# A two-layer Perceiver kernel: the spectral attention's bias as a one-row product, its spectra taken off by ScalarE, and the first half's spectra and roots moved within the last attention unit

## The chip, the cores and the metric

The kernel runs on one core of a Trainium2 chip. The metric is the device time of one execution in microseconds (us). Engines are named as the profile names them: PE is TensorE (PEld its weight loads), ACT is ScalarE, DVE is VectorE, POOL is GpSimd, SP is SyncE, which here only issues DMAs. L1563 is line 1563 of the kernel before.

## The reference

Two Perceiver layers on x [2, 256, 256] with a context [2, 4096, 256]. In order: cross attention with a Gelu, latent attention, a mixture of experts, a masked cross attention with 16 heads of 16 over the 4096 context rows, then the spectral attention that the change touches, and a mixture of expert projections with causal attention. The spectral attention, cut:

```python
def unit_projection(x):
    f = fft(x); f = f / (abs(f) + 1e-8); return ifft(f).real
query  = unit_projection(x @ Wq.T + bq)
keys   = unit_projection(x @ Wk.T + bk)
values = unit_projection(x @ Wv.T + bv)
s   = cumsum(bind(keys, values), axis=1)      # bind: product of the spectra
out = unbind(s, query)                        # product with the conjugate
x = x + out                                   # its input is layernorm(x)
```

## The kernel before, in words

Tokens lie as four tiles of 128 rows; tiles 0 and 1 are the first half (batch 0), tiles 2 and 3 the second (batch 1). Each engine has an instruction list written out by hand, and they meet at semaphores, so an engine takes its work strictly in the order of its list.

The masked cross attention runs as 32 units, one per batch and head. PE's `unit` has four turns `j`; each does score groups 2j and 2j+1 (`score_half` L1446, `score_mask` L1455) and two groups of the products with the values (`values_group` L1467); ACT takes one exponential for each half group (L953, 16 in a unit). The two last value groups of the last unit stand behind it. ACT copies the sums of a finished unit (`sums_out` L919), PE turns them (`sum_rows` L1478), DVE divides (`rows_out` L2169), and when a batch has all 16 heads, PE transposes (`o4_T` L1532), ACT copies (`o4T_out` L924) and PE projects (`y4_rows` L1542), eight products in all for a half.

From there on each half runs through: add to x (`add_psum` L2214), layer norm (`layer_stats` L1814, a power on POOL L667, `layer_scale` L1827), a transpose (`batch_norm_T` L1551) and its copy by ACT (`batch_norm_out` L930), and `spectra` (L1563), a product with the projection weights already multiplied by the Fourier matrix (`fold`), 258 columns of real and imaginary parts. k = 0, 1, 2 are keys, values and queries of the first half, k = 3, 4, 5 those of the second. Each spectrum is two tiles by two chunks of the contraction, and each of these four products stands as two MATMUL instructions in the trace. Behind a spectrum DVE adds the bias row out of a copy broadcast over the partitions and stores it (`spectrum_out` L2232), ACT squares (`squares` L939), DVE adds the two parts (`magnitude` L2240), ACT takes the root (`roots` L973). DVE then multiplies keys and values (`bind` L2245 to L2250), scales by the reciprocal sizes (`key_sizes`, `invert` L2267, `scale_keys` L2273), PE makes running sums (`running_sums` L1635, L1634), DVE multiplies with the conjugate query (`unbind`, again L2245 to L2250), PE transposes (`o5_T` L1643), ACT copies (`o5T_out` L978), PE returns by the inverse transform (`inverse` L1653), and DVE adds (`add_inverse`, L2214 again).

The first half's `spectra(0)` to `spectra(2)` run on PE inside the last unit, by the function `last_unit`, which `unit` calls in each turn after the first score group and at the turn's end. The second half waits for the last unit's sums. Behind it all stands the last stage: `project` (L1674) on PE and `gather` (L2419 to L2423) on DVE, the first `gather` behind the second half's `layer_scale(8)`. `spin` (L1052) are idle products that only keep PE running.

Of the kernel before, what the change touches and what calls it, by code (L numbers as in the profile page):

```python
# [165 lines left out]
def build(nc, a, out):  # L166
    ctx = ExitStack()
    with ctx:
# [570 lines left out]
        def _(act):  # L739
# [193 lines left out]
            def squares(k):  # L933

                b, n = k // 3, k % 3
                act.wait_ge(spec_ready, k + 1)
                if k >= 2:
                    act.wait_ge(mag_ready, k - 1)
                nc.scalar.activation(mag[:, QT * (k % 2):QT * (k % 2) + QT, :], spec[:, n, b * QT:(b + 1) * QT, :], ACT.Square)\  # L939
                   .then_inc(square_ready, 1)  # L940

            def softmax_numerators(s, u, first=False, last=False):
                for n in range(HALVES):
                    if n == 0 and last:
                        o4T_out(0)
                    if n == 4 and not first:
                        sums_out(s - 1, u - 1)
                    if n == 10 and last:
                        batch_norm_out(3, 0, T5[0])
                    if n == 14 and last:  # L950
                        squares(0)
# [8 lines left out]
            for s in range(RING):  # L960
                softmax_numerators(s, U4 - RING + s, last=(s == RING - 1))
            squares(1)
            sums_out(RING - 1, U4 - 1)
            squares(2)
            act.wait_ge(in_gate, 16 * DC + 32)
# [14 lines left out]
            roots(0)  # L980
            roots(1)
            o4T_out(1)
            roots(2)
            batch_norm_out(4, 1)
            squares(3)
            o5T_out(0)
            squares(4)
            roots(3)
            roots(4)
            squares(5)  # L990

            def row_squares(b):
# [53 lines left out]
        def _(pe):  # L1046
# [435 lines left out]
            def unit(s, u, fills, first=False, left=3, between=None):  # L1482
# [24 lines left out]
                for j in range(PAIRS):  # L1507
# [5 lines left out]
                    if between is not None:  # L1513
                        between(j, False)
                    score_group(2 * j + 1)
                    if j == PAIRS - 1 and left >= 1:
                        negmax_T(u + 1)
# [5 lines left out]
                    if between is not None:  # L1523
                        between(j, True)

# [29 lines left out]
            def spectra(k):  # L1555
# [4 lines left out]
                for q in range(QT):  # L1560
                    t = b * QT + q
                    for c in range(DC):
                        last = mm(bank[:, SPEC5[k] + q, 0:2 * NF], xnT[:, c, t * P:(t + 1) * P], fold[:, n, c, :],  # L1563
                                  start=(c == 0), stop=(c == DC - 1))
                last.then_inc(spec_psum, 1)

            def last_unit(j, whole):

                if j == 0 and whole:
                    y4_rows(0, 0)  # L1570
                    y4_rows(0, 1)
                elif j == 2 and not whole:
                    batch_norm_T(xn5[0], 5, T5[0])
                elif j == 2:
                    pe.wait_ge(in_w5, 16 * N_W5[2])
                    pe.wait_ge(xnT_ready, 4)
                    spectra(0)
                    spectra(1)
                elif j == 3 and whole:
                    spectra(2)  # L1580
# [226 lines left out]
        def _(dve):  # L1807
# [400 lines left out]
            link(v.tensor_tensor(x[:, :, :], x[:, :, :], bo4.unsqueeze(1).broadcast_to([P, TT, D]), ALU.add))  # L2208
            rows_out(RING - 1, U4 - 3)

# [5 lines left out]
            add_psum(0, Y5[0])  # L2216
            layer_stats(halves[0])
            dve.wait_ge(in_gate, 16 * DC + 32)
            v.tensor_tensor(sim2, sim6, sim6, ALU.mult).then_inc(sim_sq, 1)
# [3 lines left out]
            def rows(b):  # L2223

                return slice(b * QT, (b + 1) * QT)

            def spectrum_out(k):

                b, n = k // 3, k % 3
                o = SPEC5[k]  # L2230
                dve.wait_ge(spec_psum, k + 1)
                v.tensor_tensor(spec[:, n, rows(b), :], bank[:, o:o + 2, 0:2 * NF],  # L2232
                                brow[:, n, :].unsqueeze(1).broadcast_to([P, QT, 2 * NF]), ALU.add).then_inc(spec_ready, 1)

# [67 lines left out]

            spectrum_out(0)
            spectrum_out(1)
            magnitude(0)
            bind(0)
            magnitude(1)
            spectrum_out(2)
            rows_out(0, U4 - 2)
# [6 lines left out]
            link(v.reciprocal(col6[:, 3, :], col6[:, 2, :]))  # L2316
            key_sizes(0)
            invert(1, 0)
# [7 lines left out]
            scale_queries(0)  # L2326
            spectrum_out(3)
            unbind(0)
            spectrum_out(4)
            magnitude(3)  # L2330
# [4 lines left out]
            link(v.reciprocal(root6[:, TT:], root6[:, TT:]))  # L2335
            spectrum_out(5)
            add_inverse(0)
# [224 lines left out]
```

## Time and profile before

| | |
|---|---|
| median of 3 runs | 973.49 us (970.43 to 975.55) |
| the profiled execution | 974.15 us |
| its span, first to last instruction | 972.5 us |
| mean granted TensorE clock | 0.979 |
| busy share: PE, DVE, ACT, POOL | 94%, 61%, 46%, 10% |
| last unit of the cross attention | about 838 to 861 us of the span |
| spectral attention, both halves, to the first `gather` | to 907.3 us |
| last stage | 907.3 to 972.5 us |

A row of the timeline gives start and length in us, the engine, the line, the operation with its tensors, how many instructions it merges, and in brackets how long the engine sat idle before it and what released it. `bank` is PSUM, `region` the large SBUF tensor. Granted clock 1.00 is 2.4 GHz, 0.50 is 1.2 GHz.

### The profile page before, as it was taken

Reading aid. Unit: us, or ns where it says so; the run is one execution under the profiler, and the core shown is the slowest. Engines: PE = TensorE matmul, PEld = TensorE weight load, DVE = VectorE, ACT = ScalarE, POOL = GpSimd, SP = SyncE. Lnnn points to the kernel's source line nnn. Section 1 sums busy time; section 2 is a strip of 40 time slices with the busy share of each in tenths; the row PEclk is TensorE's granted clock in tenths of the full one; section 3 lists DMA queues with packets and bytes.
Section 4 is the critical chain, followed back from the end, with each engine's and each line's share of the span. In section 5 each row is a group of like instructions: output and inputs, shape, how many; then the busy total and the mean of one; then the engine's idle time right before and its main releaser. Section 6 shows DMA issues by size and latency. Waiting matters only on the chain.

```text
span 972.5 us, 20335 instructions
## 1 busy us (share of the span) xinstructions
PE 916.6 (94%) x7344; PEld 533.9 (55%) x7346; DVE 593.6 (61%) x1554; ACT 450.0 (46%) x836; POOL 96.9 (10%) x132
## 2 busy tenths in 40 slices
PE   5999989999989998499999999999999999978998
PEld 5888876556556556334444444444444444456657
DVE  3455343664422225478777777778777777468883
ACT  3444433541012224456666666666666666632102
POOL 1222321000501110100000000000000000010000
PEclk9999998999999999889999999999999999989999
DMA  7844689507118208974445544555445552710000
GB/s 260 272 164 162 223 320 304 165 1 260 58 24 119 77 21 210 248 193 75 68 64 81 80 67 64 69 80 78 64 59 80 80 71 70 132 44 1 1 0 22
DMA packets 76358, 107.75 MB, mean 111 GB/s; under 512 B 27084, under 2 KB 62512, under 8 KB 72275
## 3 DMA queue, kind: packets, MB, share of 16 engines
q1 hardware_dynamic: 71147, 91.65, 43.6%
q0 software_dynamic: 4960, 14.96, 4.2%
q8 instruction: 34, 0.56, 0.3%
q10 hardware_dynamic: 200, 0.44, 0.2%
q14 instruction: 17, 0.14, 0.0%
HBM read 84.21 MB, written 21.03 MB: 108 GB/s over the span
## 4 chain that ended last, share of the span: by engine, by line
PE 81%; DVE 8%; DMA 4%; ACT 2%; POOL 2%; issue 2%; SPq 0%; ACTq 0%; POOLq 0%; DVEq 0%
PE bank L1446 14%; PE bank L1467 13%; PE bank L1455 9%; PE bank L1424 7%; PE bank L1091 5%; PE bank L1306 5%; PE bank L1104 5%; PE bank L1334 3%; PE bank L1674 2%; PE bank L1186 1%; PE bank L1079 1%; PE bank L1736 1%; PE bank L1195 1%; PE bank L1478 1%; DMA keys_split<-region 1%
## 5 line engine op out<-in xcount | busy, mean ns | idle before, releaser
L953 ACT ACTIVATE region<-bank 128x512 f32<-128x512 f32 x512 | 278.0, 595 | 161.1 <-PE bank L1455 161.1
L2140 DVE CUSTOM_DVE_ANT_0 xnT<-bank,region 128x1024 bf16<-128x1024 f32 x128 | 156.2, 1220 | 81.3 <-issue 81.3
L1446 PE MATMUL bank<-region 128*128 (+1 forms) x1024 | 158.8, 277 | 2.1 <-ACT region L953 1.5
L2140 DVE CUSTOM_DVE_ANT_0 region<-bank,region 128x1024 bf16<-128x1024 f32 x128 | 156.3, 1221 | 0.9 <-issue 0.5
L1467 PE MATMUL bank<-region 128*32 128x256 f32 x2048 | 138.8, 385 | 0.0
L1446 PEld LDWEIGHTS bank<-region 128*128 128x128 bf16 x1024 | 69.8, 98 | 120.6 <-issue 59.6
L1455 PE MATMUL bank<-region,identb 64*64 64x512 bf16 x1024 | 105.7, 403 | 0.0
L1424 PE MATMUL bank<-region,xnT 64*128 64x512 bf16 x248 | 76.2, 387 | 8.8 <-DMA xnT<-region 8.5
L1467 PEld LDWEIGHTS bank<-region 128*32 128x32 f32 x2048 | 58.8, 109 | 40.5 <-ACT region L953 14.5
L1426 PE MATMUL bank<-region,xnT 64*128 64x512 bf16 x248 | 76.2, 387 | 0.0
L1306 PE MATMUL bank<-region 128*64 (+1 forms) x192 | 59.8, 466 | 2.2 <-DVE region L2053 1.6
L1091 PE MATMUL bank<-xnT,region 128*128 128x256 f32 x256 | 58.1, 380 | 0.3 <-ACT xnT L743 0.3
L722 POOL COPY region<-region 128x512 f32<-128x512 f32 x30 | 18.5, 617 | 398.5 <-PE bank L1467 398.5
L1104 PE MATMUL bank<-region 128*128 128x256 f32 x256 | 57.9, 379 | 0.0
L1455 PEld LDWEIGHTS bank<-region,identb 64*64 64x64 bf16 x1024 | 28.9, 103 | 48.9 <-issue 48.0
L1091 PEld LDWEIGHTS bank<-xnT,region 128*128 128x128 f32 x256 | 48.7, 191 | 6.9 <-issue 0.4
L1912 DVE TENSOR_TENSOR region<-region 128x1024 bf16<-128x1024 f32 x16 | 19.6, 1226 | 52.1 <-ACT region L784 52.1
L1104 PEld LDWEIGHTS bank<-region 128*128 128x128 f32 x256 | 47.5, 190 | 5.8
L779 ACT ACTIVATE region<-bank 128x512 f32<-128x512 f32 x32 | 19.1, 598 | 63.7 <-PE bank L1091 63.7
L677 POOL DMA_DIRECT2D keys_split<-region x48 | 35.9, 749 | 102.2 <-DVE region L1912 102.2
L1674 PE MATMUL bank<-region,xnT 128*128 128x384 f32 x128 | 43.8, 490 | 1.0 <-ACT xnT L930 0.8
L1306 PEld LDWEIGHTS bank<-region 128*64 128x64 f32 (+1 forms) x192 | 29.6, 159 | 27.0 <-issue 6.3
(376 smaller groups left out, 1196.8 us busy)
## 6 DMA issues: line engine op xcount, KB each, us to landing
region<-keys_split SPq DMA_DIRECT2D x224, 128.0 KB, 4.9
region<-in_ctx SPq DMA_DIRECT2D x32, 512.0 KB, 7.0
keys_split<-region POOLq DMA_DIRECT2D x48, 256.0 KB, 4.4
region<-in_L_ffn_we_gate SPq DMA_DIRECT2D x8, 688.0 KB
region<-in_L_ffn_we_up SPq DMA_DIRECT2D x8, 688.0 KB
region<-in_mask_1x1xSxS_ik SPq DMA_DIRECT2D x1, 4096.0 KB, 15.9
region<-in_L_ffn_we_down SPq DMA_DIRECT2D x8, 512.0 KB
mask_kept<-region SPq DMA_DIRECT2D x1, 2048.0 KB, 12.1
```

The costliest lines, as they stand in the source:

```text
L677: pool.dma_start(keys_dram[part, bass.ds(b * D, D), bass.ds((2 * j + s) * CH, CH)] .rearrange("(c p) f -> p c f", p=P), split[s][:, part, ...
L953: nc.scalar.activation(prob4[n % PROBS].rearrange("p a b -> p (a b)"), bank[:, SCORE4[n], :], ACT.Exp, scale=SCALE4).then_inc(exp4_ready, 1)
L1091: last = mm(bank[:, 2 + p, t * S:(t + 1) * S], ctxT[s % 2][:, d, f:f + P], xnT[:, d, b * S:(b + 1) * S], start=(d == 0), stop=(d == DC - 1))
L1104: last = mm(bank[:, 4 + q, 0:D], geluT[p][:, t, q * P:(q + 1) * P], ctx_in[s][:, 2 * p + t, :], start=(s + p + t == 0), stop=(s == SLOTS1 ...
L1306: last = mm(bank[0:rows_by(i), 2 * w + n, 0:FH], xbT[i % 2][:, c, 0:rows_by(i)], packed3[:, bass.ds(owner, 1), at3:at3 + FH].rearrange("p ...
L1424: mm(bank[:, b, :], qmax4[s][0:64, q * P:(q + 1) * P], slab[s][0:64, c * CH:(c + 1) * CH], start=True, stop=True)\
L1426: mm(bank[:, b + 1, :], qmax4[s][64:P, q * P:(q + 1) * P], slab[s][64:P, (c + 1) * CH:(c + 2) * CH], start=True, stop=True).then_inc(max_p ...
L1446: mm(bank[:, SCORE4[n], k * S:(k + 1) * S], slab[s][:, t * P:(t + 1) * P], qT4[:, bass.ds(u, 1), :].rearrange("p o q -> p (o q)"), start=( ...
L1455: last = mm(bank[o, SCORE4[2 * g + k], :], identb[i, i], maskT[i, 4 * g + 2 * k:4 * g + 2 * k + 2, :].rearrange("p a b -> p (a b)"), start ...
L1467: last = mm(bank[32 * k:32 * k + 32, 7, 0:S], vaug[s % 2][:, 4 * g + k, :], prob4[(2 * g + k // 2) % PROBS][:, k % 2, :], start=(g == 0), ...
L1674: last = mm(bank[:, DEEP6[k % len(DEEP6)], 0:2 * QKV], xnT[:, c, t * P:(t + 1) * P], w6[:, c, e:e + 2, :].rearrange("p a b -> p (a b)"), s ...
L2140: v.tensor_tensor_reduce(out=junk[q], in0=bank[:, 3 + 2 * q:5 + 2 * q, :].rearrange("p a b -> p (a b)"), in1=maskN[:, q, 2 * c * CH:2 * (c ...
```

## The change

1. The bias comes in as one more product: `ones[0:1, :]` (one row of 128 ones) with the bias row `brow[0:1, n, :]` of 258 columns opens each accumulation, two for a spectrum, twelve in all. As each float32 product stands as two MATMULs in the trace, that is 24 instructions.
2. DVE's `spectrum_out` (six of them) is gone. ACT squares straight from PSUM and then copies the spectrum out, two ACT instructions where one was.
3. In the last unit, PE's pieces stand earlier: `y4_rows` in turn 0 between the two score groups, `batch_norm_T` in turn 1, `spectra(0)` and `spectra(1)` at the end of turn 1, `spectra(2)` at the end of turn 2.
4. On ACT, `squares(0)` and `squares(1)` with their copies stand among the last unit's exponentials; behind the last exponential come `roots(0)`, `roots(1)`, then `squares(2)` and its copy, and only then `sums_out` of the last unit.
5. On DVE, `rows_out` of unit 29 stands behind the first half's statistics, `magnitude(1)` ahead of `bind(0)`, and `key_sizes(0)` ahead of the `rows_out` of the last two units.

```diff
             def squares(k):
-                b, n = k // 3, k % 3
-                act.wait_ge(spec_ready, k + 1)
+                act.wait_ge(spec_psum, k + 1)
                 if k >= 2:
                     act.wait_ge(mag_ready, k - 1)
-                nc.scalar.activation(mag[:, QT * (k % 2):QT * (k % 2) + QT, :], spec[:, n, b * QT:(b + 1) * QT, :], ACT.Square)\
-                   .then_inc(square_ready, 1)
+                nc.scalar.activation(mag[:, QT * (k % 2):QT * (k % 2) + QT, :], bank[:, SPEC5[k]:SPEC5[k] + 2, 0:2 * NF],
+                                     ACT.Square).then_inc(square_ready, 1)
+
+            def spectrum_out(k):
+
+                b, n = k // 3, k % 3
+                nc.scalar.activation(spec[:, n, b * QT:(b + 1) * QT, :], bank[:, SPEC5[k]:SPEC5[k] + 2, 0:2 * NF], ACT.Copy)\
+                  .then_inc(spec_ready, 1)
...
             for s in range(RING):
                 softmax_numerators(s, U4 - RING + s, last=(s == RING - 1))
-            squares(1)
-            sums_out(RING - 1, U4 - 1)
-            squares(2)
...
             roots(0)
             roots(1)
+            squares(2)
+            spectrum_out(2)
+            sums_out(RING - 1, U4 - 1)
             o4T_out(1)
             roots(2)
             batch_norm_out(4, 1)
-            squares(3)
+            for k in (3, 4):
+                squares(k)
+                spectrum_out(k)
             o5T_out(0)
-            squares(4)
             roots(3)
             roots(4)
             squares(5)
+            spectrum_out(5)
...
                 for q in range(QT):
                     t = b * QT + q
+                    mm(bank[:, SPEC5[k] + q, 0:2 * NF], ones[0:1, :], brow[0:1, n, :], start=True, stop=False)
                     for c in range(DC):
                         last = mm(bank[:, SPEC5[k] + q, 0:2 * NF], xnT[:, c, t * P:(t + 1) * P], fold[:, n, c, :],
-                                  start=(c == 0), stop=(c == DC - 1))
+                                  start=False, stop=(c == DC - 1))
                 last.then_inc(spec_psum, 1)
...
-                if j == 0 and whole:
+                if (j, part) == (0, 0):
                     y4_rows(0, 0)
                     y4_rows(0, 1)
-                elif j == 2 and not whole:
+                elif (j, part) == (1, 1):
                     batch_norm_T(xn5[0], 5, T5[0])
-                elif j == 2:
+                elif (j, part) == (1, 2):
                     pe.wait_ge(in_w5, 16 * N_W5[2])
                     pe.wait_ge(xnT_ready, 4)
                     spectra(0)
                     spectra(1)
-                elif j == 3 and whole:
+                elif (j, part) == (2, 2):
                     spectra(2)
...
-            spectrum_out(0)
-            spectrum_out(1)
             magnitude(0)
+            magnitude(1)
             bind(0)
-            magnitude(1)
-            spectrum_out(2)
+            key_sizes(0)
             rows_out(0, U4 - 2)
             rows_out(None, U4 - 1)
...
-            spectrum_out(3)
             unbind(0)
-            spectrum_out(4)
             magnitude(3)
             bind(1)
             magnitude(4)
...
-            spectrum_out(5)
             add_inverse(0)
```

ACT at the end of the last unit, before: L953 are exponentials, L939 the squares, L919 the copy of the last unit's sums, L973 the roots with their table load, L924 the copy of the transposed rows for the second half's projection.

```order
L953 ACTIVATE region<-bank 128x512 [waits score4] x2
L939 ACTIVATE region<-region 128x516 [waits spec_ready]
L919 ACTIVATE region<-bank 128x290 [waits o4_unit,pv_psum]
L939 ACTIVATE region<-region 128x516 [waits mag_ready,spec_ready]
L966 ACTIVATE region<-region 128x16 [waits in_gate]
L973 ACT_TABLE_LOAD
L973 ACTIVATE region<-region 128x258 [waits mag_ready] x2
L924 ACTIVATE xnT<-bank 128x2x256 [waits o4T_psum]
```

And of the change, at the same place (L962 exponentials, L938 squares, L944 the copy of the spectrum, L979 roots):

```order
L962 ACTIVATE region<-bank 128x512 [waits score4] x4
L972 ACTIVATE region<-region 128x16 [waits in_gate]
L979 ACT_TABLE_LOAD
L979 ACTIVATE region<-region 128x258 [waits mag_ready] x2
L938 ACTIVATE region<-bank 128x516 [waits mag_ready,spec_psum]
L944 ACTIVATE region<-bank 128x516
L919 ACTIVATE region<-bank 128x290 [waits o4_unit,pv_psum]
L924 ACTIVATE xnT<-bank 128x2x256 [waits o4T_psum]
```

The copy of the last unit's sums (L919) stood ahead of the table load and the roots, and now stands behind them, behind a square and behind a copy.

PE in the last turn of the last unit and behind it, before (L1446 and L1455 scores, L1467 values, L1563 a spectrum, L1478 the turn of the sums):

```order
L1446 MATMUL bank<-region 128x256
L1455 MATMUL bank<-region,identb 64x512 x4
L1467 MATMUL bank<-region 32x256 [waits exp4_ready]
L1467 MATMUL bank<-region 32x256 x3
L1467 MATMUL bank<-region 32x256 [waits exp4_ready]
L1467 MATMUL bank<-region 32x256 x3
L1563 MATMUL bank<-region,xnT 128x258 [waits spec_ready]
L1563 MATMUL bank<-region,xnT 128x258 x3
L1467 MATMUL bank<-region 32x256 [waits exp4_ready]
```

Of the change, `spectra(2)` and what follows it (L1575 the one-row product, L1577 the spectrum's own, L1457 and L1466 scores):

```order
L1575 MATMUL bank<-region,ones 128x258 [waits spec_ready]
L1577 MATMUL bank<-region,xnT 128x258 x2
L1575 MATMUL bank<-region,ones 128x258
L1577 MATMUL bank<-region,xnT 128x258 x2
L1457 MATMUL bank<-region 128x256 [waits exp4_ready]
L1457 MATMUL bank<-region 128x256
L1457 MATMUL bank<-region 128x256 [waits exp4_ready]
L1457 MATMUL bank<-region 128x256
L1466 MATMUL bank<-region,identb 64x512 x4
```

`spectra(2)` stood behind the last scores and now stands ahead of the last two score groups, and two one-row products have joined its four.

PE in the second half, of the change, from `batch_norm_T` to `o5_T`:

```order
L1564 MATMUL bank<-ident,xn 128x128 [waits xn_ready]
L1564 MATMUL bank<-ident,xn 128x128 x3
L1575 MATMUL bank<-region,ones 128x258 [waits xnT_ready]
L1577 MATMUL bank<-region,xnT 128x258 x2
L1575 MATMUL bank<-region,ones 128x258
L1577 MATMUL bank<-region,xnT 128x258 x2
L1575 MATMUL bank<-region,ones 128x258 [waits spec_ready]
L1577 MATMUL bank<-region,xnT 128x258 x2
L1575 MATMUL bank<-region,ones 128x258
L1577 MATMUL bank<-region,xnT 128x258 x2
L1657 MATMUL bank<-ident,region 128x128 [waits o5_ready]
```

Nothing has changed its place here; `spectra(3)` and `spectra(4)` are twelve products where they were eight.

## Rows read from the trace of the kernel before

**Rows 1.** The page: busy time and share of the span by engine.

```profile
PE 916.6 (94%) x7344; PEld 533.9 (55%) x7346; DVE 593.6 (61%) x1554; ACT 450.0 (46%) x836; POOL 96.9 (10%) x132
```

**Rows 2.** The chain that ended last, 838 to 975 us: start, length, what.

```profile
859.75 1.05 PE bank L1467 x16
...
861.88 1.28 ACT L973
863.17 0.73 ACT region L973 x2
864.43 3.61 PE bank L1542 x8
868.07 0.70 DVE x L2214
...
873.51 3.82 PE bank L1563 x8
877.43 0.70 DVE region L2232
```

**Rows 3.** Stretches: length, busy PE, PEld, DVE, ACT, POOL, granted clock, DMA share, GB/s.

```profile
861.00:864.00 3.00, 1.72 (x12) 1.38 (x12) 1.57 (x8) 2.97 (x7) 0.00 (x0) 1.00 0.19 62
864.00:868.00 4.00, 3.57 (x9) 2.81 (x10) 3.26 (x5) 0.69 (x2) 0.00 (x0) 0.58 0.00 0
873.00:878.00 5.00, 4.49 (x11) 3.56 (x12) 1.79 (x4) 0.46 (x1) 0.68 (x1) 0.50 0.00 0
878.00:880.00 2.00, 1.62 (x7) 1.07 (x5) 1.93 (x6) 0.63 (x1) 0.00 (x0) 0.92 0.00 0
880.00:907.00 27.00, 21.86 (x122) 17.46 (x122) 24.36 (x78) 6.40 (x14) 2.33 (x3) 1.00 0.00 1
```

**Rows 4.** Timeline of PE: spectra, `y4_rows`, `o4_T`, inverse.

```profile
842.08 1.99 PE L1542 MATMUL bank<-woutT,xnT 128*128 128x256 f32 x8
850.86 3.75 PE L1563 MATMUL bank<-region,xnT 128*128 128x258 f32 x16
862.40 0.66 PE L1532 MATMUL bank<-ident,xn 128*128 128x128 f32 x4
864.43 3.59 PE L1542 MATMUL bank<-woutT,xnT 128*128 128x256 f32 x8 [1.38 <-ACT xnT L924]
873.51 6.11 PE L1563 MATMUL bank<-region,xnT 128*128 128x258 f32 x16 [0.69 <-ACT xnT L930]
883.01 1.89 PE L1653 MATMUL bank<-region 128*128 128x256 f32 x8
```

**Rows 5.** Timeline of ACT around the last unit's end.

```profile
856.92 1.09 ACT L953 ACTIVATE region<-bank 128x512 f32<-128x512 f32 x2
860.82 0.41 ACT L919 ACTIVATE region<-bank 128x290 f32<-128x290 f32 x1 [2.29 <-PE bank L1467]
863.80 0.58 ACT L924 ACTIVATE xnT<-bank 128x512 f32<-128x512 f32 x1
```

**Rows 6.** Groups by line and form: other heights, and the instructions that change engine.

```profile
L1186 PE MATMUL bank<-region x64: 377/379/483, 165.0 to 210.9; 65*128 65x256 f32 x64
L1736 PE MATMUL bank<-region 128*128 128x256 f32 x64 | 14.8, 382 | 0.0
L2232 DVE TENSOR_TENSOR region<-bank,region 128x516 f32<-128x516 f32 x6 | 4.2, 694 | 9.5 <-PE bank L1563 9.5
L939 ACT ACTIVATE region<-region 128x516 f32<-128x516 f32 x6 | 3.8, 634 | 5.4 <-DVE region L2232 5.4
L930 ACT ACTIVATE xnT<-bank 128x512 f32<-128x512 f32 x4 | 2.4, 598 | 15.7 <-PE bank L1551 15.7
```

**Rows 7.** Timeline of DVE behind the last unit.

```profile
881.56 0.42 DVE L2245 TENSOR_TENSOR region<-region 128x258 f32<-128x258 f32 x1
885.53 0.68 DVE L2214 TENSOR_TENSOR x<-x,bank 128x512 f32<-128x512 f32 x1
907.27 0.42 DVE L2419 TENSOR_SCALAR region<-bank,weight 128x192 f32<-128x192 f32 x1
```

More of the change, by code:

```diff
@@ L947, in softmax_numerators @@
                         sums_out(s - 1, u - 1)
+                    if n == 8 and last:
+                        batch_norm_out(3, 0, T5[0])
+                        squares(0)
+                        spectrum_out(0)
                     if n == 10 and last:
-                        batch_norm_out(3, 0, T5[0])
-                    if n == 14 and last:
-                        squares(0)
+                        squares(1)
+                    if n == 12 and last:
+                        spectrum_out(1)
                     act.wait_ge(score4, HALVES * u + n + 1)
@@ L1513, in unit @@
                     if between is not None:
-                        between(j, False)
+                        between(j, 0)
                     score_group(2 * j + 1)
+                    if between is not None:
+                        between(j, 1)
                     if j == PAIRS - 1 and left >= 1:
@@ L1523, in unit @@
                     if between is not None:
-                        between(j, True)
+                        between(j, 2)
             def o4_T(b):
@@ L1561, in spectra, with last_unit @@
                     t = b * QT + q
+                    mm(bank[:, SPEC5[k] + q, 0:2 * NF], ones[0:1, :], brow[0:1, n, :], start=True, stop=False)
                     for c in range(DC):
                         last = mm(bank[:, SPEC5[k] + q, 0:2 * NF], xnT[:, c, t * P:(t + 1) * P], fold[:, n, c, :],
-                                  start=(c == 0), stop=(c == DC - 1))
+                                  start=False, stop=(c == DC - 1))
                 last.then_inc(spec_psum, 1)
-            def last_unit(j, whole):
-                if j == 0 and whole:
+            def last_unit(j, part):
+                if (j, part) == (0, 0):
                     y4_rows(0, 0)
                     y4_rows(0, 1)
-                elif j == 2 and not whole:
+                elif (j, part) == (1, 1):
                     batch_norm_T(xn5[0], 5, T5[0])
-                elif j == 2:
+                elif (j, part) == (1, 2):
                     pe.wait_ge(in_w5, 16 * N_W5[2])
@@ L2208, in _ @@
             link(v.tensor_tensor(x[:, :, :], x[:, :, :], bo4.unsqueeze(1).broadcast_to([P, TT, D]), ALU.add))
-            rows_out(RING - 1, U4 - 3)
             def add_psum(b, o):
@@ L2217, in _ @@
             layer_stats(halves[0])
+            rows_out(RING - 1, U4 - 3)
             dve.wait_ge(in_gate, 16 * DC + 32)
@@ L2225, in rows @@
                 return slice(b * QT, (b + 1) * QT)
[L2227 to L2233, printed above, removed]
             def magnitude(k):
@@ L2316, in _ @@
             link(v.reciprocal(col6[:, 3, :], col6[:, 2, :]))
-            key_sizes(0)
             invert(1, 0)
```

## The prediction

> **What bounds the kernel now.** The page comes first: PE is busy for 94% of the span, DVE for 61%, ACT for 46% [rows 1]. That is an average over stages, so the chain that ended last is read next, and in it only the stretch that the change touches [rows 2]. From the last unit's last values (859.75) the chain goes over ACT's table load and first two roots, the second half's projection on PE (864.43, L1542), DVE's addition at 868.07, spectra(3) at 873.51, and DVE's copy of that spectrum at 877.43. The stretches [rows 3] show two things: the granted clock was 1.00 up to 864 and 0.58 between 864 and 868, behind a stretch in which PE had been busy 1.72 of 3.00 us, 0.50 between 873 and 878 and 0.92 between 878 and 880; and from 880 to 907 DVE is busy 24.36 of 27 us. So the last unit is bound by PE, the middle (861 to 880) by hand-overs between ACT, PE and DVE, and 880 to 907 nearly by DVE alone. I read the change as a set of shifts of three moments: y4 of the second half done (868.02, where DVE's addition waits), bind of the second half (DVE L2245 at 881.56), and the first inverse added (885.53) [rows 7]. The last of these is followed by work that the change doesn't touch: it reaches the first gather at 907.27 [rows 7], and the last stage goes on from there. What shifts 885.53 shifts the end.
>
> **1. The one-row products in the last unit.** Each adds two MATMULs of 258 columns. No row has a height of 1. Two rows of different heights say that height doesn't count: 65 rows by 256 columns took a median of 379 ns, 128 rows by 256 columns a mean of 382 [rows 6]. Back to back, 16 instructions of a spectrum took 3.75 us, 0.234 each [rows 4]. I take 0.234 as the price of one; the lower bound is 0 (it streams beside its neighbours), and the upper is the half-clock price, 3.59/8 = 0.45 [rows 4], where the clock is down. Three spectra have 12 such instructions: 2.8 us. In the last unit PE has hardly a gap, so all of it lies on the path: the last values end at 860.80 + 2.8 = 863.6 [rows 2].
>
> **2. Where the last exponentials end.** Before, they ended at 856.92 + 1.09 = 858.01 [rows 5], with spectra(2) behind them. Now the last four wait for scores behind all three spectra: 858.01 + 2.8 + 1.9 (the own eight instructions of spectra(2), 8 x 0.234) = 862.7. The earlier y4_rows and batch_norm_T cost nothing: the same products in another order, beside exponentials that ACT has room for (it waited 2.29 us at the end of the unit [rows 5]). The new wait in ACT's list, squares(0) ahead of exponential 8, holds the exponentials back by nothing either, since the scores they need come behind spectra(1) on PE.
>
> **3. ACT ahead of the sums.** From 862.7: the gates' exponential 0.2, the table load 1.28, two roots 0.73 [rows 2], then squares(2) and its copy. These read PSUM: a copy of 512 columns from there took 598 ns, a square of 516 from SBUF 634 [rows 6], so 0.6 each, bounds 0.5 and 0.7. Together 3.4 us, and sums_out (0.41) ends at 866.5, where before it ended at 861.23 [rows 5]. That is 5.3 us later. The roots that were to come earlier come later too: 864.2 against 863.17, so key_sizes doesn't pay it back.
>
> **4. From the sums to y4.** Before, from 861.23 to 868.02: 6.8 us, of which the copy L924 lost 0.74 behind the roots (the transposes ended at 863.06, the copy began at 863.80 [rows 4, 5]). Now ACT is free there: 6.1 us, with the projection at half clock as before (3.59 us where it is 1.99 at full clock [rows 4]). y4 is done at 866.5 + 6.1 = 872.6, so this moment is **4.5 us** later. DVE's own list (two rows_out, magnitude, invert, scale_keys behind the sums) is done at about 872, just ahead of it.
>
> **5. Second half.** Call DVE's addition T (868.07 before, 872.6 now). Spectra(3) starts at T + 5.4, as before. Spectra(3) and (4) are 24 instructions where they were 16. Before, 16 took 6.11 us: 4.7 at half clock (to about 878.2) held ten, and six more at 0.234 took 1.4. With the same half-clock stretch the other 14 take 3.3: 8.0 us, to T + 13.4. Then square, copy and hand-overs, 1.4: bind(1) can start at T + 14.8, where it was T + 13.5. DVE has nothing to do meanwhile: unbind(0) no longer waits for spectra(3), is early, and DVE then idles. That is where the DVE work taken off is given back. PE goes on with o5_T 0.5, spectra(5) 12 x 0.234 = 2.8, inverse 1.9 [rows 4] and 0.2 of hand-over: T + 18.8. DVE's road to the same addition is 14.8 + (17.46 - 13.49) - 0.6 = 18.2, its spectrum_out(5) saved, so PE ends last. Before it was 885.53 - 868.07 = 17.46. So **1.35 us** later. Behind that nothing is shorter; ACT's last square and copy lie under DVE's work.
>
> The Trainium skill (TensorE: Matmul & The Clock Gate, What's actually happening) says that the half rate is the default and that activity on PE releases it; by it the longer wait before the sums (3 us now, from 863.6 to 866.5) makes a low clock at y4 surer, and eight more products make the rise behind spectra(3) no later. By that rule alone the sum stays; without the release, spectra(3) and (4) would take 24 x 0.45 = 10.8 us instead of 8.0. The granted clock of 0.50 in 873 to 878 and 1.00 from 880 [rows 3] agrees with it.
>
> **Sum.** 4.5 + 1.35 = 5.85 us on the profiled execution, 974.15 us: 980.0. The median of the runs is 0.66 lower, so 979.3. Nearly all of it is the price of the one-row products: 12 of them ahead of the sums, 8 in spectra(3) and (4), 4 in spectra(5), 24 x 0.234 = 5.6. What ACT's new order costs and what the early unbind gives almost cancel.
>
> **Rivals.** (a) *The one-row product is nearly free.* The mechanism: one row of weights and one row of data, loaded and streamed beside the tall product next to it. Then the sum is 5.85 - 5.6 = +0.2: 973.7. Not slower. It decides from about 0.19 us per instruction: under that the change is within 4.9 us. Against it: equal times for 65 and 128 rows [rows 6]; for it, only that nothing as low as 1 is shown. 0.14. (b) *The clock is held.* More products and less pause between them keep 1.00 at y4 and through spectra(3) and (4): 3.59 - 1.99 = 1.6 less, and 24 x 0.234 = 5.6 instead of 8.0, 2.4 less; DVE's list then ends last at the first place, which leaves about 1.0 of the 1.6. +2.5: 976.0, no measurable change. Against it: the pause before the sums grows. 0.15. (c) *VectorE's relief decides.* With (a) and (b) both, DVE is the bound of 868 to 907, and its three spectrum_out (3 x 0.6) and its wait for PE at 877.43 go: about -3, 970.5. This is the other side, and it needs an instruction under 0.1 us. 0.05. (d) *The clock stays low throughout*, from the sums to the end of spectra(4), because the pauses between PE's pieces are longer: 10.8 instead of 8.0, +8.6: 982.1. For it: the clock fell at 864 behind a stretch with PE busy 1.72 of 3.00 us [rows 3], and now PE stands still for 3 us there. The Trainium skill's same page says that pauses bring the default back, which is this rival's rule. 0.15. (e) The change doesn't do what it says, as where a wait on the early DMAs of fold or of the gates shows inside the unit: its price is open, 0.03.
>
> **How the numbers follow.** My forecast, +4.3 to +7.3 with 979.3 in the middle, has 0.48. A measurement of this kernel tells about 0.5% (4.9 us) from no change. Slower by more: three quarters of the forecast (0.36), all of (d) and (e), 0.54. Faster by more needs (c) and luck on top: 0.04. The rest, 0.42, is within 0.5%. The range goes from 973.5, which takes in (b) and the free product's edge, to 983.0, which takes in (d).
>
> **What would show it.** In the profile of the changed kernel: the one-row products at 0.23 us each back to back; last values at 863 to 864; PE idle for about 3 us before the turn of the sums, ACT's copy of them ending 5 us later than before; DVE idle ahead of magnitude(3) and of bind(1), 2 us or more each; the first gather at about 913; the last stage as long as before. I am wrong if the one-row products take under 0.15 us, if the first gather stands before 910, or if the clock is 1.00 between the sums and spectra(4).

## The result, and the profile after

The change is slower: 995.09 us (median of 4 runs, 986.72 to 998.9) against 974.52 us for the kernel before (970.43 to 976.99), a ratio of 1.0204 with a 95% interval of 1.0127 to 1.028. The forecast was 979.3 us with a range to 983.0, so the sign was right and the size was not. The profiled execution took 986.72 us, span 985.0, mean granted clock 0.974. It is the fastest of the four, so what the profile shows (12.6 us over the profile of before) is less than the 20.6 us between the medians. What is left is taken up behind the prediction's steps. The ratios leave out slow runs, among them those that gave the profiles of e3 (996.23 us) and e7 (998.58 us) and one run of e1 that took 4847.93 us.

The page of the changed kernel, busy time by engine (against [rows 1]):

```profile
PE 928.1 (94%) x7368; PEld 538.8 (55%) x7370; DVE 589.7 (60%) x1548; ACT 452.8 (46%) x842; POOL 96.9 (10%) x132
```

PE has 24 more instructions and is busy 11.5 us longer, which is far more than 24 times 0.234 us. The chain that ended last shows where (against [rows 2]; start, length, what):

```profile
870.92 0.70 DVE x L2227
...
881.13 1.15 PE bank L1575 x2
882.29 2.02 PE bank L1577 x4
...
894.68 3.31 PE bank L1667 x8
898.09 0.70 DVE x L2227
```

Lines of the changed kernel: L1575 is the one-row product, L1577 the spectrum's own, L1489 the turn of the sums, L1545 `o4_T`, L1657 `o5_T`, L1667 the inverse, L979 ACT's table load and roots, L938 and L944 its square and new copy. The addition at 870.92 is followed by the layer norm and the transpose; from spectra(3) at 875.91 to the addition at 898.09 the chain is all PE, with five of the six one-row pairs at 1.15 us and only the first at 0.70. The stretches (against [rows 3]; length, busy PE, PEld, DVE, ACT, POOL, granted clock, DMA share, GB/s) show why:

```profile
864.00:870.00 6.00, 5.31 (x18) 4.46 (x19) 4.05 (x11) 0.91 (x2) 0.00 (x0) 0.50 0.02 7
871.00:877.00 6.00, 2.94 (x14) 1.85 (x13) 5.14 (x12) 0.60 (x1) 3.57 (x2) 1.00 0.00 0
878.00:897.00 19.00, 19.00 (x40) 11.51 (x41) 5.30 (x15) 4.49 (x9) 0.00 (x0) 0.50 0.00 0
898.00:919.00 21.00, 17.71 (x102) 13.74 (x101) 18.61 (x61) 3.92 (x9) 2.34 (x3) 1.00 0.00 1
```

For 19 us PE has not one idle moment in the records, and all that time the clock is 0.50, that is 1.2 GHz. Before, it was back at 1.00 by 880 [rows 3]. DVE waits for it three times, in its timeline (start, length, then what; in brackets the idle time before it and what released it; against [rows 7]):

```profile
881.80 0.43 DVE L2246 TENSOR_TENSOR region<-region 128x258 f32<-128x258 f32 x1 [1.98 <-ACT region L938]
888.64 0.43 DVE L2251 TENSOR_TENSOR region<-region 128x258 f32<-128x258 f32 x1 [6.41 <-ACT region L944]
898.09 0.69 DVE L2227 TENSOR_TENSOR x<-x,bank 128x512 f32<-128x512 f32 x1 [6.12 <-PE bank L1667]
```

L2246 is magnitude(3), L2251 bind(1), L2227 the addition of the first inverse. And PE's timeline, in the last unit at full clock and in the second half at half clock (against [rows 4]; the tile forms are weights, then data):

```profile
853.67 0.70 PE L1575 MATMUL bank<-region,ones 1*128 1x258 f32 x2
854.29 1.14 PE L1577 MATMUL bank<-region,xnT 128*128 128x258 f32 x4
855.36 0.70 PE L1575 MATMUL bank<-region,ones 1*128 1x258 f32 x2
...
863.92 1.04 PE L1489 MATMUL bank<-summer,region 128*128 128x17 f32 x4 [2.73 <-ACT region L919]
...
865.65 1.09 PE L1545 MATMUL bank<-ident,xn 128*128 128x128 f32 x4
...
887.27 1.06 PE L1657 MATMUL bank<-ident,region 128*128 128x128 f32 x4
888.26 1.22 PE L1575 MATMUL bank<-region,ones 1*128 1x258 f32 x2
889.42 2.09 PE L1577 MATMUL bank<-region,xnT 128*128 128x258 f32 x4
891.44 1.22 PE L1575 MATMUL bank<-region,ones 1*128 1x258 f32 x2
...
894.47 3.50 PE L1667 MATMUL bank<-region 128*128 128x256 f32 x8
```

**One measure for all runs.** Every kernel of this study, the one before included, scatters by several us upstream of the change, so I compare profiles by one stretch: from the last unit's first `o4_T` to the first gather. It is the part that the change touches. The last stage behind it is 65.2 us long before (972.5 less 907.3) and after (985.0 less 919.8). Before, the stretch runs from 838.3 to 907.3, **69.0 us**; after, from 834.2 to 919.8, **85.6 us** (ends rounded to 0.1, so a stretch is good to 0.1). The forecast of +5.85 is 74.85 us in this measure. Its start stands in the groups of instructions by line; this is the row of before, and behind it the row of after:

```profile
L1532 PE MATMUL bank<-ident,xn x4: 272/273/327, 838.3 to 838.7; 128*128 128x128 f32 x4
```

```profile
L1545 PE MATMUL bank<-ident,xn x4: 272/272/330, 834.2 to 834.5; 128*128 128x128 f32 x4
```

### The profile page after: what moved, and what is told of

Its sections match the earlier page's. It is cut to its first block, busy times and chain, and to the rows that moved or that the text cites. A ratio compares the mean times of both kernels' runs of the same rounds, so it can differ in the third digit from the quotient of the medians.

```text
span 985.0 us, 20383 instructions
## 1 busy us (share of the span) xinstructions
PE 928.1 (94%) x7368; PEld 538.8 (55%) x7370; DVE 589.7 (60%) x1548; ACT 452.8 (46%) x842; POOL 96.9 (10%) x132
## 4 chain that ended last, share of the span: by engine, by line
PE 83%; DVE 6%; DMA 3%; SPq 3%; ACT 2%; issue 1%; another core or an unknown queue 1%; POOL 0%; ACTq 0%; DVEq 0%
PE bank L1457 14%; PE bank L1478 12%; PE bank L1466 9%; PE bank L1435 7%; PE bank L1317 6%; PE bank L1115 5%; PE bank L1102 4%; PE bank L1345 3%; PE bank L1285 2%; PE bank L1688 2%; PE bank L1577 2%; PE bank L1197 1%; PE bank L1750 1%; PE bank L1206 1%; PE bank L1489 1%
## 5 line engine op out<-in xcount | busy, mean ns | idle before, releaser
L962 ACT ACTIVATE region<-bank 128x512 f32<-128x512 f32 x512 | 277.9, 595 | 162.9 <-PE bank L1466 162.9
L1457 PE MATMUL bank<-region 128*128 (+1 forms) x1024 | 158.4, 277 | 2.1 <-ACT region L962 1.5
L1478 PE MATMUL bank<-region 128*32 128x256 f32 x2048 | 138.6, 385 | 0.0
L1457 PEld LDWEIGHTS bank<-region 128*128 128x128 bf16 x1024 | 69.7, 98 | 120.5 <-issue 59.6
L1466 PE MATMUL bank<-region,identb 64*64 64x512 bf16 x1024 | 105.7, 403 | 0.0
L1478 PEld LDWEIGHTS bank<-region 128*32 128x32 f32 x2048 | 58.9, 109 | 40.3 <-ACT region L962 14.5
L1466 PEld LDWEIGHTS bank<-region,identb 64*64 64x64 bf16 x1024 | 28.9, 103 | 48.8 <-issue 47.9
L1317 PEld LDWEIGHTS bank<-region 128*64 128x64 f32 (+1 forms) x192 | 30.3, 163 | 32.9 <-issue 12.6
L2093 DVE TENSOR_TENSOR region<-region,bank 128x344 f32<-128x344 f32 x24 | 12.3, 513 | 55.2 <-PE bank L1321 36.3
```

Source lines behind the costliest of these rows:

```text
L1317: last = mm(bank[0:rows_by(i), 2 * w + n, 0:FH], xbT[i % 2][:, c, 0:rows_by(i)], packed3[:, bass.ds(owner, 1), at3:at3 + FH].rearrange("p ...
L1457: mm(bank[:, SCORE4[n], k * S:(k + 1) * S], slab[s][:, t * P:(t + 1) * P], qT4[:, bass.ds(u, 1), :].rearrange("p o q -> p (o q)"), start=( ...
L1466: last = mm(bank[o, SCORE4[2 * g + k], :], identb[i, i], maskT[i, 4 * g + 2 * k:4 * g + 2 * k + 2, :].rearrange("p a b -> p (a b)"), start ...
L1478: last = mm(bank[32 * k:32 * k + 32, 7, 0:S], vaug[s % 2][:, 4 * g + k, :], prob4[(2 * g + k // 2) % PROBS][:, k % 2, :], start=(g == 0), ...
```

## The experiments

Three theories. **A:** products that hold fewer rows than their neighbours keep a clock that has fallen at half, though PE is busy. **B:** the new order's pauses keep it low. **C:** the one-row product is only dearer than I took it for, and the clock follows other things. All results first; "low" is the time at half clock between 840 and 925 us of the profiled execution, worked out from its mean granted clock there (two decimals, so good to 1 us); in most profiles it has a first part behind the last unit and in some a second from about spectra(3) on. Stretch and low are read from one profile each; the ratio is against the kernel before and over several runs.

| run | stretch, us | low, us | ratio (95%) |
|---|---|---|---|
| before | 69.0 | 10.2 | 1 |
| the change | 85.6 | 27.2 | 1.0204 (1.0127 to 1.028) |
| e1 bias on 128 rows | 74.7 | 13.6 | 1.0019 (0.9986 to 1.0052) |
| e2 change, no bias | 67.4 | 6.8 | 0.9978 (0.9939 to 1.0017) |
| e3 before, with one-row bias | 83.3 | 30.6 | 1.009 (1.0046 to 1.0134) |
| e4 before, with 128-row bias | 71.3 | 3.4 | 1.0025 (0.9989 to 1.0061) |
| e5 the change again | 75.2 | 3.4 | 1.0163 (1.0127 to 1.0199) |
| e6 bias on 32 rows | 86.8 | 34 | 1.0185 (1.0135 to 1.0236) |
| e7 change, with spins | 86.3 | 27.2 | 1.0118 (1.0054 to 1.0181) |
| e8 before, with spins | 65.9 | 3.4 | 0.9956 (0.9925 to 0.9988) |
| e9 128 rows in the second half only | 75.8 | 17 | 1.0096 (1.0056 to 1.0136) |
| e10 128 rows in the first half only | 84.7 | 30.6 | 1.0143 (1.0074 to 1.0211) |
| e11 128 rows and spins | 71.0 | 3.4 | 1.0052 (1.0016 to 1.0087) |
| e12 before, second spin only | 66.4 | 3.4 | 1.0017 (0.9983 to 1.005) |
| e13 bias on 64 rows | 86.8 | 34 | 1.0157 (1.0115 to 1.0199) |
| e14, e15 as e9, one run each | 73.8, 76.6 | 7, 14 | no ratio: 980.69 and 993.24 us |
| e16 as e8, again | 65.8 | 3.4 | 0.9969 (0.9937 to 1.0001) |

**e1 and e2: the bias with all 128 rows, and no bias at all.** In e1 the same sum is spread over 128 rows; all else is the change. In e2 the product is left out, so the bias is missing from what is computed.

```diff
+share = sb("share", [P, P]);  nc.gpsimd.memset(share[:, :], 1.0 / 128)
-mm(bank[...], ones[0:1, :], brow[0:1, n, :], start=True, stop=False)
+mm(bank[...], share[0:128, :], brow[0:128, n, :], start=True, stop=False)
```

> The change with its bias product 128 rows tall (a tile of 1/128 against the bias row on all 128 partitions) in place of one row; same number of instructions, same order. Theory A (one-row products keep TensorE's clock at half although PE is busy): the half-clock stretch behind spectra(3) ends within 6 us of its start, as before, and the time is 977 to 982 us, near my forecast. Theory B (the new order's pauses hold the clock down, whatever the height): as the change, 987 to 999 us, half clock for about 20 us. Theory C (only the longer time of a one-row pair, 0.62 us against 0.47, counts): about 2 us below the change.

> The change without any bias product (the bias of the spectral attention is left out). It shows what the new order and ScalarE's copies do alone. Theory A: no long half-clock stretch; 972 to 977 us, by my working +0.2 us on before. Theory B: the pauses are the same, so the clock stays down and the time is over 982 us.

With the same number of instructions of the same 258 columns, e1's stretch is 10.9 us shorter than the change's, and its time can't be told from before. PE's timeline of e1 in the second half:

```profile
884.78 1.93 PE L1579 MATMUL bank<-region,xnT 128*128 128x258 f32 x4
886.50 1.07 PE L1577 MATMUL bank<-region,share 128*128 128x258 f32 x2
...
890.81 0.60 PE L1577 MATMUL bank<-region,share 128*128 128x258 f32 x2
891.24 1.03 PE L1579 MATMUL bank<-region,xnT 128*128 128x258 f32 x4
```

The clock was down here too when spectra(3) began (1.93 us for four), and came back within the third tile, by 890: the pair at 890.81 took 0.60 us. The fall came at 883.1, just ahead of spectra(3), and lasted 6.8 us. C wanted e1 about 2 us under the change, and it is 10.9 us under it in the stretch: more than the price of the pairs is at work. e2 stands at 0.9978: the new order by itself costs nothing that can be measured. In e2's profile the clock fell only once, behind the last unit, so it doesn't show how a second fall would have ended; against B stands e1, which has the change's order and pauses and gets its clock back.

**e3 and e4: the kernel before, with the bias product alone added.** Order and `spectrum_out` as before, DVE's addition turned into a plain copy.

```diff
+mm(bank[...], ones[0:1, :], brow[0:1, n, :], start=True, stop=False)    # e3; e4: share[0:128, :], brow[0:128, n, :]
-v.tensor_tensor(spec[...], bank[...], brow[...].broadcast_to(...), ALU.add)
+v.tensor_copy(spec[...], bank[...])
```

> The kernel before, with its order and DVE's exits, but with the one-row bias product on PE, DVE copying where it added. Theory A: the half clock stays for 10 us or more from spectra(3) on, 984 us or more. Theory B: the order is the old one, so the clock comes back as before: 24 instructions at 0.23 to 0.31 us, of which the six behind the last unit's start count, 977 to 981 us.

> As the run before (old order, bias product on PE, DVE copies), with the product 128 rows tall. Both theories: 976 to 981 us; theory A expects this 5 us or more under the one-row form, theory B within 2 us of it.

The one-row product brings the long low clock into the old order as well, which is the second thing against B. With 128 rows it is gone: e4's clock fell too, 0.7 us into spectra(3), and was back after 3.4 us. A stretch of e3, then two of e4 (columns as above):

```profile
900.00:906.00 6.00, 6.00 (x13) 3.94 (x14) 2.68 (x8) 0.70 (x3) 0.00 (x0) 0.50 0.00 0
```

```profile
874.00:877.30 3.30, 3.30 (x10) 2.56 (x9) 0.54 (x2) 0.00 (x0) 0.00 (x0) 0.50 0.02 5
877.50:884.00 6.50, 5.67 (x28) 4.68 (x27) 5.79 (x15) 2.06 (x4) 0.00 (x0) 1.00 0.00 0
```

**e5: the change a second time.**

> The change unaltered, as the measure for this group's chip. All theories: 1.01 to 1.025 of before; a half-clock stretch of 15 us or more behind spectra(3) in most executions.

This profile shows that the fall is not certain. PE's timeline of e5, the same program, spectra(3) to (5):

```profile
876.27 0.66 PE L1564 MATMUL bank<-ident,xn 128*128 128x128 f32 x4 [2.37 <-DVE xn L1841]
877.61 0.70 PE L1575 MATMUL bank<-region,ones 1*128 1x258 f32 x2 [0.69 <-ACT xnT L930]
...
886.53 0.70 PE L1575 MATMUL bank<-region,ones 1*128 1x258 f32 x2
888.14 1.89 PE L1667 MATMUL bank<-region 128*128 128x256 f32 x8
```

The pauses ahead are those of after (2.37 and 0.69 us; there 2.38 and 0.69), and the clock stayed at 1.00. So one-row products don't pull a full clock down at once; where it doesn't fall, the stretch is 75.2 us, within 0.4 us of the forecast. The timed runs of e5, 978.73 to 996.87 us, are as wide as that difference and more, and the other four took 989.85 us or more: this profile, with the fastest run, is the exception.

**e6 and e13: 32 and 64 rows.** As e1, with `share[0:32, :]` at 1/32 and `share[0:64, :]` at 1/64.

> The change with the bias product 32 rows tall (a tile of 1/32 against the bias row on 32 partitions). If the height of the product is what keeps the clock down, 32 of 128 rows is still short: half clock for 10 us or more in most executions and 1.005 to 1.02 of before, between the one-row form and the 128-row form (1.002). If only height 1 is special, about 1.002.

> The bias product on 64 rows of 1/64 and 64 rows of the bias. If the rows of a product decide by degrees whether a fallen clock comes back (1 and 32 rows: stretch of 86 and 87 us; 128 rows: 75 us): 73 to 78 us from the last unit's first o4_T to the first gather, 1.000 to 1.008 of before. If anything short of 128 rows holds the clock down: 83 us or more there, 1.012 or more.

There are no degrees. Both cost what the one-row product costs. PE's timeline of e13, at full and at half clock:

```profile
848.19 0.70 PE L1577 MATMUL bank<-region,share 64*128 64x258 f32 x2
...
882.50 1.23 PE L1577 MATMUL bank<-region,share 64*128 64x258 f32 x2
```

**e7, e8, e11, e12, e16: the pauses filled.** Idle products on PE: `spin(1, 5)` (10 MATMULs) behind the second half's `o4_T` and `spin(1, 9)` (18) ahead of its `batch_norm_T`. e7 adds them to the change, e8 to the kernel before, e11 to e1; e12 has the second alone; e16 repeats e8.

```diff
 o4_T(1)
+spin(1, 5)
...
 running_sums(0)
+spin(1, 9)
 batch_norm_T(xn5[1], 6)
```

> The change plus idle tall products (10 MATMULs ahead of the second half's y4 rows, 18 ahead of its batch_norm_T) in pauses of PE, so that PE comes to spectra(3) without a pause. Theory A (one-row products pull the clock down or hold it down by themselves): the clock still falls within spectra(3) to (5) or stays down there, and less than 4 us is gained on the change. Theory B (the pause ahead makes it fall): the clock is 1.00 through the spectra and 8 us or more is gained, down to 1.003 of before or under.

> The kernel before plus the same idle products at the same two places. If the half clock of 864 to 868 and 871 to 878 costs what my rows say (1.6 and 2.4 us), up to 3 us is gained, 0.997 to 0.999 of before; if the clock falls at the same moments although PE is kept running, nothing is gained, 1.000 to 1.002.

> The change with 128-row products and the idle tall products in the two pauses. If these gain in the new order what they gained in the old one (0.4%), 0.996 to 1.000 of before; the old order with them, 0.9956, stays ahead of it by the price of the bias products.

> The kernel before with the idle products only ahead of batch_norm_T of the second half, to tell which of the two pauses pays. If it is the low clock in spectra(3) and (4) (2.4 us by my rows against 1.6 at y4): 0.996 to 0.998 of before; if it is y4, 0.999 to 1.001.

> The kernel before with the two spins, a second time and with more rounds. If its gain is real: 0.994 to 0.999 of before, and 65 to 67 us from the last unit's first o4_T to the first gather (before: 69). If the first result was scatter: 0.999 to 1.002.

B expected e7 to bring the change back, to 1.003 or less. The ratio is 1.0118, and the profile has the long low clock; PE's timeline of e7:

```profile
883.95 2.17 PE L1063 MATMUL bank<-ident 128*128 128x128 f32 x18
886.48 0.66 PE L1564 MATMUL bank<-ident,xn 128*128 128x128 f32 x4 [0.36 <-DVE xn L1843]
887.82 0.70 PE L1575 MATMUL bank<-region,ones 1*128 1x258 f32 x2 [0.69 <-ACT xnT L930]
888.45 1.73 PE L1577 MATMUL bank<-region,xnT 128*128 128x258 f32 x4
```

No pause from 883.95 on is over 0.69 us, and yet the clock falls 1 us into spectra(3) and stays down until the inverse. So a long pause just ahead isn't needed. That isn't the whole of e7, though: two of its four runs (983.01 and 984.6 us) had a mean clock of 0.983 and 0.981. As an estimate, (1 - clock) times 2 times the span, that is 33 and 37 us at half clock in all, and as every profile of this study has 24 us or more of it up to the last unit, a stretch of 20 us has hardly any room in them. Of the nine runs of the change and e5 the same holds for one (e5's 978.73, 31 us). Whether the spins make the fall rarer is open. In the kernel before the spins do work (e8): its stretches show the clock at 1.00 where it was 0.62 and 0.81 without them, over the same two windows; first e8, then before.

```profile
870.00:876.00 6.00, 5.12 (x28) 4.04 (x27) 4.98 (x9) 1.23 (x2) 2.68 (x1) 1.00 0.01 3
876.00:882.00 6.00, 4.49 (x25) 4.05 (x26) 5.70 (x16) 1.84 (x4) 0.00 (x0) 1.00 0.00 0
```

```profile
870.00:876.00 6.00, 3.60 (x10) 2.74 (x11) 3.49 (x7) 0.60 (x1) 3.57 (x2) 0.62 0.00 0
876.00:882.00 6.00, 4.85 (x20) 3.76 (x19) 4.43 (x12) 1.17 (x3) 0.00 (x0) 0.81 0.00 0
```

e8 and e16 are the version that stands ahead of both kernels: 3.1 and 3.2 us less in the stretch, 0.9956 (more than the 0.997 to 0.999 expected) and 0.9969 in time. The second interval just reaches 1.0001, so the gain of 3 to 4 us is likely rather than proven. e12 gives 2.6 us in the stretch, but 1.0017 in time, outside both of its expectations. e11 missed its expectation (0.996 to 1.000) with 1.0052. Its stretch is 5.1 us longer than e8's, 0.21 for each of its 24 tall products, though the order of the work differs too between the two; e1's rows below give the same price, 0.43 us a pair. That is near my 0.234 each.

**e9, e10, e14, e15: tall rows in one half only.** `if b == 1:` takes the tall product, otherwise the one-row product (e9, e14, e15); e10 has it the other way about.

> The change with 128-row bias products in the second half's three spectra and one-row products in the first half's. Theory A in its present form (a clock that has fallen does not come back while one-row products stand among the tall ones; the first half's spectra run in the last unit at full clock and do no harm): about the 128-row form, 1.001 to 1.006 of before, and a half-clock stretch in the spectra of under 8 us. If one-row products anywhere do the harm: 1.01 or more.

> The reverse: one-row products only in the second half's three spectra. Theory A: as the change, 1.011 to 1.02 of before, half clock of 10 us or more in most executions. If the harm is done in the last unit: 1.001 to 1.006.

> One more profile of the kernel with the tall bias in the second half only, whose time (1.0096) was above that with all 24 tall (1.0019). If its excess lies in this stretch: 79 us or more from the last unit's first o4_T to the first gather. If it came from upstream: 73 to 77 us.

> A third profile of the same kernel as the run before, with the same two expectations: 79 us or more from the last unit's first o4_T to the first gather if its excess lies in this stretch, 73 to 77 us if it came from upstream.

One-row products in the last unit, where the clock is 1.00, leave the stretch at 73.8 to 76.6 us over three profiles; one-row products in the second half alone, where the clock has fallen, make it 84.7 in the one profile of e10. Two stretches of e10, then of e15:

```profile
880.00:903.00 23.00, 23.00 (x48) 13.88 (x49) 7.25 (x20) 4.49 (x9) 0.58 (x1) 0.50 0.00 1
904.00:910.00 6.00, 4.16 (x27) 3.23 (x26) 5.49 (x14) 1.44 (x6) 1.50 (x2) 1.00 0.00 0
```

```profile
891.00:897.00 6.00, 5.66 (x13) 4.53 (x14) 4.04 (x10) 0.38 (x2) 0.95 (x1) 0.50 0.01 3
898.00:904.00 6.00, 6.00 (x32) 5.23 (x31) 2.90 (x8) 1.97 (x5) 0.00 (x0) 1.00 0.00 0
```

So place matters: in these profiles the same twelve instructions cost about 9 us more in the second half than inside the dense unit. The times don't show it by themselves. e9's 1.0096 lies above its expectation (1.001 to 1.006), and its interval overlaps that of e10. In the profiles of e9 and e15 more than half of the excess came from upstream: e9's last unit began at 846.6 us, e15's at 849.8, e14's at 840.0, against 838.3 before. For e9's other runs this isn't shown. I haven't found why: ten of the profiles (e1, e2, e3, e7, e9, e10, e12, e14, e15, e16) have 17 us or more at half clock between 100 and 200 us, where that of before has 7, so this is no property of the one kernel.

**All profiles together.** Wherever the clock fell about the second half's `batch_norm_T` and spectra(3) with short products in the second half (the change, e3, e6, e7, e10, e13), it stayed down for 20 to 24 us and came back 1.8 to 3.4 us into the inverse, the first long run of products of one height. Wherever it fell there without them (before, e1, e4, e9, e15), it was back after 3.4 to 6.8 us. In e5, with short products, it didn't fall there, nor in e2, e8, e11, e12, e14 and e16 without them. So a fall needs no short products: in e4 and e9, with tall ones, it came 0.7 us into spectra(3). What goes with the short ones is how long it lasts.

## Why the prediction was wrong

By its own steps, each moment counted from the last unit's first `o4_T` (838.3 before, 834.2 after):

| moment | before | forecast | after |
|---|---|---|---|
| last values end | 22.5 | 25.3 | 27.0 |
| `sums_out` ends | 22.9 | 28.2 | 29.7 |
| y4 done, DVE's addition T | 29.8 | 34.3 | 36.7 |
| spectra(3) starts | 35.2 | 39.7 | 41.7 |
| bind(1) starts | 43.3 | 49.1 | 54.4 |
| first inverse added | 47.2 | 53.1 | 63.9 |
| first gather | 69.0 | 74.85 | 85.6 |

**Step 1, the price, mis-sized.** A one-row pair and the four products behind it take 1.70 us from start to start (853.67 to 855.36), where four alone take 0.90, by the old spectrum's 16 from 850.86 [rows 4] to the next product of before:

```profile
854.45 0.60 PE L1446 MATMUL bank<-region 128*128 128x256 bf16 x4
```

So a pair costs 0.80, not 0.47: 0.62 for itself and the rest for the four behind it. A spectrum is two of these, 3.39 us, before 1.80. Three of them make 4.8 us, and the last values stand at +4.5, not +2.8. The two heights that I compared [rows 6] were each among products of their own height; the change alternates heights. The weight loads say what is different. Of the change, then of e1:

```profile
853.66 0.29 PEld L1575 LDWEIGHTS bank<-region,ones 1*128 1x128 f32 x2 [0.41 <-issue]
854.29 0.73 PEld L1577 LDWEIGHTS bank<-region,xnT 128*128 128x128 f32 x4 [0.34 <-issue]
855.36 0.29 PEld L1575 LDWEIGHTS bank<-region,ones 1*128 1x128 f32 x2 [0.34 <-issue]
```

```profile
854.96 0.41 PEld L1577 LDWEIGHTS bank<-region,share 128*128 128x128 f32 x2
855.39 0.84 PEld L1579 LDWEIGHTS bank<-region,xnT 128*128 128x128 f32 x4
```

With equal heights the gap between load groups is 0.04 us or less; at each change of height, in either direction, the load waits 0.34 us for nothing that the profile shows. The Trainium skill (TensorE: Matmul & The Clock Gate, Architectural detail: the array is 16× 32×32, not 1× 128×128) says that PE's queue can pull weight loads ahead of products in flight. e1's rows look like that, the change's don't at these borders.

**Step 2 moved by step 1's price, step 3 held.** The last exponentials ended 6.6 us later than before (26.3 against 19.7 from the first `o4_T`), forecast 4.7. From the last values to the end of `sums_out` it took 2.7 us, forecast 2.9. ACT's table load, roots, square and copy cost what they were costed at. PE stood 2.73 us ahead of the sums, forecast about 3.

**Step 4, small miss.** From the sums to y4: 7.0 us, forecast 6.1. The low clock began before the turn of the sums instead of behind it: `o4_T` took 1.09 us where it took 0.66 [rows 4].

**Step 5, the failed step.** It assumed "the same half-clock stretch" as before, 4.7 us from the start of spectra(3). Measured, the clock fell at 877.3 and stayed at half until 897.7, 20.4 us. From T to the first inverse's addition it took 27.2 us, forecast 18.8. The excess of 8.4 is: spectra(3) and (4) 11.4 us (875.91 to 887.27) for 8.0, +3.4; spectra(5) 6.2 us (888.26 to 894.47) for 2.8, +3.4; `o5_T` and the inverse at half clock +2.1; the start 0.4 earlier, and rounding. Rival (d) had the mechanism's half: a clock held low, 0.15, 982.1 us. It let the low clock end with spectra(4) and laid it to the pause. Taken through spectra(5) (12 x 0.22 more) and the inverse (1.6 more), it gives 982.1 + 4.2 = 986.3, outside my range. What ended it too soon was the belief that busy products bring the clock back. The Trainium skill (same page, What's actually happening) states just this, that activity releases the half rate; the trace doesn't agree as far as busy time goes, with 19.00 of 19 us busy at 0.50. With tall products in the same place it does agree (e1, back after 6.8 us).

**The rest of the sum.** From the first inverse's addition to the gather it took 21.7 us before and after, as forecast. Of the surplus of 10.8 us over the forecast in this stretch, e5 gives the clock's part: the same program without the second fall is 75.2, so 10.4 us are the clock, and the dearer pairs are about made up for in e5 by the full clock through spectra(3) and (4) (10.8 us forecast for the three spectra, 10.2 by 6 x 1.70). Rivals (a) and (c) fell: no pair was cheap. Rival (b) didn't come either, though in e5's profile its second place, spectra(3) and (4) at 1.00, did. The order of the work, the part that the diff makes most of, comes out at +0.2 us forecast and nothing measurable in e2.

**Outside the stretch.** The median is 15.8 us over the forecast, the stretch accounts for 10.8. The profiled execution reached the last unit 4.1 us sooner than that of before (834.2 against 838.3), which leaves 6.7 us over the 980.0 forecast for it, and it is the fastest of its four. By their mean clock (0.974, 0.967, 0.961, 0.964, in the estimate used for e7) the four runs had 51, 65, 78 and 72 us at half clock; the profiled one had the least. Where the others had theirs no profile shows, so this part of the slowdown goes with the clock and its place stays open.

**What stands and what is open.** That the height of the bias product sets the price of the pair is shown by the rows of e1 and e13 at full clock, and that it sets how long a fallen clock stays down by the profiles of e1, e3, e4, e6, e10 and e13. The ratios of e1, e4, e6, e10 and e13 say the same; those of e3 (1.009, short) and e9 (1.0096, tall in the second half) don't tell short from tall. Why the clock stays down is argued only: "busy" in the records includes the waits for loads, since a pair and its four products at half clock take 3.18 us with short rows (888.26 to 891.44) and 2.58 with tall (e1, 886.50 to 889.08), so the array does the same work more thinly. Whether it is the shortness or the change of height was not separated: no run had short products among short ones at a fallen clock. Open too is what makes the clock fall in spectra(3) in one execution and not in another, why in e7 it fell without a long pause, and how often it falls: nearly all kernels have one profile.

## What to carry to other kernels

Before folding a bias into a product, ask whether the short product stands among tall ones where the clock may have fallen: there twelve instructions cost some 9 us on top of their own 4.8, since the clock came back only in the next long run of tall products. Spread over all 128 rows (each 1/128 of the sum) the same bias cost 0.21 us an instruction, and the clock recovered within the spectra. And a price read from rows of one height, each among its like, isn't the price of alternating them.

## What the runs showed of the hardware

- A float32 product with 1, 32 or 64 rows of contraction among products of 128 rows: the pair takes 0.62 us from start to start at full clock where 128 rows take 0.43, and the four products behind it 1.07 instead of 0.87. Between 1, 32 and 64 rows there was no difference.
- A clock at 0.50 for 19 us of unbroken PE records (878 to 897), and as long or longer in e3, e6, e7, e10 and e13. With tall products in the same place it was back after 3.4 to 6.8 us (e4: 874.0 to 877.4, e1: 883.1 to 889.9).
- Idle products in two pauses took the half-clock time of the kernel before from 10.2 to 3.4 us, and 3 us off the stretch (e8, e16).
